# Turns of the identity in TensorE's pauses, and another order in the first expert tile

## The reference, cut to what matters

```python
def gat_layer(x, W, a_src, a_dst, bias, src, dst, heads, out_c, concat):
    h = (x @ W).reshape(n, heads, out_c)
    al_s, al_d = einsum(h, a_src), einsum(h, a_dst)
    e = leaky_relu(al_s[src] + al_d[dst], 0.2)
    ex = exp(e - segment_max(e, dst)[dst])
    alpha = ex / (segment_sum(ex, dst)[dst] + 1e-16)
    return segment_sum(h[src] * alpha, dst) + bias
...
x = x + gat_layer(elu(gat_layer(layernorm(x), heads=8, out_c=96)), heads=1, out_c=768)
# experts: 4 groups of 8, of which each token takes 2 groups and 4 experts in each
combine = softmax(top2(xf @ Wg + bg)) * softmax(top4(xf @ We + be))     # xf = layernorm(x)
y += (gelu(xf @ W1[g, e] + b1) @ W2[g, e] + b2) * combine[:, g, e]      # 768 -> 384 -> 768
```

## Time and profile before

| what | value |
|---|---|
| median of 3 runs | 1533.72 us (1532.51 to 1535.9) |
| profiled execution, its own time | 1535.3 us |
| its span, first to last instruction | 1533.3 us |
| mean granted clock of TensorE | 0.954 |
| busy: TensorE, DVE, ScalarE, POOL | 1362.5, 1160.9, 738.2, 503.2 us |

### The profile page before, as it was taken

The page is one execution under the profiler, slowest core; times in us unless marked ns, Lnnn a source line. Parts: engine busy times, 40 slices in busy tenths (PEclk is TensorE's granted clock), DMA queues, the critical chain, the costliest instruction groups (busy, mean ns, idle before and its releaser), DMA issues. The chain is left out here.

```text
span 1533.3 us, 31074 instructions
## 1 busy us (share of the span) xinstructions
PE 1362.5 (89%) x7643; PEld 1135.7 (74%) x7654; DVE 1160.9 (76%) x1823; ACT 738.2 (48%) x1171; POOL 503.2 (33%) x557
## 2 busy tenths in 40 slices
PE   6798888888778779889966999999999999999995
PEld 3555656633323339889966899999999999999995
DVE  6489999899999977858877576555566655888882
ACT  2565565255555552422224355444454544666662
POOL 1000000003333410032324454555555544655563
PEclk9999999799999989999976999999999999999998
DMA  6300001041222223233566887767778876889953
GB/s 231 137 18 9 18 21 68 18 177 61 72 94 72 68 54 130 62 104 105 125 183 219 238 215 197 192 163 162 169 197 211 200 193 154 214 268 271 257 126 49
DMA packets 102255, 211.68 MB, mean 138 GB/s; under 512 B 19318, under 2 KB 58486, under 8 KB 102082
## 3 DMA queue, kind: packets, MB, share of 16 engines
q1 hardware_dynamic: 79186, 142.06, 28.1%
q0 software_dynamic: 22240, 66.69, 21.7%
q10 hardware_dynamic: 784, 2.36, 0.4%
HBM read 164.14 MB, written 54.93 MB: 143 GB/s over the span
## 5 line engine op out<-in xcount | busy, mean ns | idle before, releaser
L976 PE MATMUL ps_o<-prob,h_head 128*97 128x512 f32 (+1 forms) x480 | 188.0, 529 | 51.5 <-DVE prob L918 51.5
L2050 POOL DMA_INDIRECT out_nodes<-y,to_index x92 | 159.7, 1736 | 148.3 <-issue 94.0
L2351 PE MATMUL ps_h<-e_hi,e_xt_hi 128*128 (+1 forms) x546 | 193.5, 354 | 7.1 <-ACT e_xt_hi L2169 3.7
L2336 PE MATMUL ps_y<-e_hi,e_ht_hi 128*128 (+1 forms) x546 | 193.1, 354 | 3.9 <-DVE e_ht_lo L2268 2.2
L976 PEld LDWEIGHTS ps_o<-prob,h_head 128*97 128x97 f32 x480 | 73.3, 165 | 165.6 <-issue 89.9
L2351 PE MATMUL ps_h<-e_lo,e_xt_hi 128*128 (+1 forms) x546 | 185.8, 340 | 0.0
L2336 PE MATMUL ps_y<-e_hi,e_ht_lo 128*128 (+1 forms) x546 | 184.8, 338 | 0.0
L2336 PE MATMUL ps_y<-e_lo,e_ht_hi 128*128 (+1 forms) x546 | 184.7, 338 | 0.0
L2234 DVE TENSOR_TENSOR e_lo<-raw,e_hi (+1 forms) x189 | 176.1, 952 | 7.6 <-ACT e_hi L2177 6.7
L2187 ACT ACTIVATE y<-ps_y,gate 128x768 f32 (+1 forms) x91 | 82.2, 903 | 196.7 <-DMA out_nodes<-y,to_index 100.4
L810 ACT ACTIVATE score<-score,al_col 128x1250 f32<-128x1250 f32 x80 | 106.0, 1335 | 98.7 <-DVE score L861 98.7
(11 more groups left out here) (346 smaller groups left out, 3037.7 us busy)
## 6 DMA issues: line engine op xcount, KB each, us to landing
raw<-in_ew SPq DMA_DIRECT2D x192, 384.0 KB, 5.8
w_room<-rel_dram SPq DMA_DIRECT2D x14, 640.0 KB, 4.5
b_all<-in_eb SPq DMA_DIRECT2D x32, 192.0 KB
al_src<-al_dram SPq DMA_DIRECT2D x1, 5000.0 KB, 14.8
xs<-in_x SPq DMA_DIRECT2D x5, 768.0 KB, 12.5
x_in_t<-in_x SPq DMA_DIRECT2D x10, 384.0 KB, 3.5
out_nodes<-x SPq DMA_DIRECT2D x10, 384.0 KB, 4.1
table<-xf SPq DMA_DIRECT2D x10, 384.0 KB, 2.6
```

The costliest lines, as they stand in the source:

```text
L976: turn = nc.tensor.matmul(ps_o[u][0:C1 + 1, c, 0:WID[c]], h_head[:, u, t, :], prob[:, t % 2, 512 * c:512 * c + WID[c]], start=(t == 0), st ...
L2050: nc.gpsimd.indirect_dma_start(out, bass.IndirectOffsetOnAxis(to_index[:, w:w + 1], 0), y[:, w, :], None, bounds_check=NP - 1, oob_is_err= ...
L2336: last = nc.tensor.matmul(ps_y[:, half, 0:HALF], a, b[:, bass.ds(u, 1), at:at + HALF].rearrange("p o d -> p (o d)"), start=(m == 0), stop= ...
L2351: nc.tensor.matmul(ps_h[:, 0:HID], xt_hi[:, c, :], b[:, bass.ds(e % 2, 1), c * HID:(c + 1) * HID] .rearrange("p o m -> p (o m)"), start=(c ...
```

## The change

A helper turns the identity into a PSUM bank that nothing reads. It is called at five places: 16 times in stage 1 after the first tile's products, 24 times before and 16 times behind the last `add_terms`, 8 times and 18 times in stage 5 around the last bias and the last list, and 3 times at the start of stage 6. In stage 6 the third list moves: on TensorE from behind the products of tile 0 to ahead of them, on DVE ahead of the low parts of expert 0's W2. DVE's first tile is written out in a function of its own: third list, match of the fourth, copy of tile 1, two low parts of W2, bias, `keep`, last low part of W2, split of tile 1, copy of tile 2, low part of the GELU, three low parts of expert 1's W1, match of the fifth.

```diff
+def turn_nothing(nc, s, to, times):
+    for n in range(times):
+        nc.tensor.transpose(to, s.ident[:, :], s.ident[:, :])
...
                 for t in range(NT):
+                    if t == 1:
+                        turn_nothing(nc, s, ps_al[:, 2, HALF:512], 16)
                     if t + 2 < NT:
                         turn_x(t + 2)
...
+                turn_nothing(nc, s, first_steep[:, 0:P], 24)
                 add_terms(H1 - 1, 1, last=True).then_inc(al_summed, 1)
+                turn_nothing(nc, s, first_steep[:, 0:P], 16)
...
                 turn_gates(NT - 1)
+                turn_nothing(nc, s, ps_l[:, 0:P], 8)
                 weigh_bias(NT - 1)
                 list_now(2)
+                turn_nothing(nc, s, ps_l[:, 0:P], 18)
...
+                def first_tile():
+                    keep_third()
+                    match(AHEAD - 1, 2, rows_made)
+                    keep_rows(1)
+                    weights(0, 1, (0, 1))
+                    dve.wait_ge(h_summed, 1)
+                    dve.wait_ge(b1_in, 16)
+                    nc.vector.tensor_tensor(h_in[:, :], ps_h[:, 0:HID], b1_all[:, 0, :], ALU.add).then_inc(biased, 1)
+                    keep(0)
+                    weights(0, 1, (2,))
+                    split_x(1)
+                    keep_rows(2)
+                    dve.wait_ge(h_hi_made, 1)
+                    nc.vector.tensor_tensor(ht_lo[:, :, :]..., ALU.subtract).then_inc(h_lo_made, 1)
+                    weights(1, 0, range(3))
+                    match(AHEAD, 3, rows_made)
+
                 def tile(k, e, which, start, last):
+                    if start:
+                        first_tile()
+                        return
...
                 split_x(0)
-                weights(0, 1, range(3))
                 over_tiles(dve, "dve_tiles", tile, alone)
...
                     if start:
-                        pe.wait_ge(third_made, 1)
-                        list_tokens(nc, s, ps_l).then_inc(third_listed, 1)
+                        pe.wait_ge(rows_made, 1)
+                        pe.wait_ge(third_kept, 2)
+                        list_tokens(nc, s, ps_l).then_inc(listed, 1)
                     turn_x(k + 1)
-                    if head and not last:
+                    if head and not last and not start:
                         pe.wait_ge(rows_made, e + 1)
-                        if start:
-                            pe.wait_ge(third_kept, 2)
                         list_tokens(nc, s, ps_l).then_inc(listed, 1)
...
                 turn_x(0)
+                pe.wait_ge(third_made, 1)
+                list_tokens(nc, s, ps_l).then_inc(third_listed, 1)
+                turn_nothing(nc, s, ps_y[:, 0, 0:P], 3)
                 n = over_tiles(pe, "pe_tiles", tile)
```

More of the change, by code:

```diff
@@ L2237, in weights @@
                                                 ALU.subtract).then_inc(made, 1)
+                def first_tile():
[11 more added lines that the diff above has]
+                    dve.wait_ge(h_hi_made, 1)
+                    nc.vector.tensor_tensor(ht_lo[:, :, :].rearrange("p k n -> p (k n)"), ps_t[:, 0:HID],
+                                            ht_hi[:, :, :].bitcast(F32).rearrange("p k n -> p (k n)"),
+                                            ALU.subtract).then_inc(h_lo_made, 1)
+                    weights(1, 0, range(3))
+                    match(AHEAD, 3, rows_made)
                 def tile(k, e, which, start, last):
+                    if start:
+                        first_tile()
+                        return
                     head = which == 0
@@ L2242, in tile @@
                         weights(e + 1, 0, (0, 1))
-                    if start:
-                        keep_rows(k + 1)
                     dve.wait_ge(h_summed, k + 1)
@@ L2247, in tile @@
                         dve.wait_ge(b1_in, 16 * e + 16)
-                    if not start:
-                        dve.wait_ge(gelued, k)
+                    dve.wait_ge(gelued, k)
                     nc.vector.tensor_tensor(h_in[:, :], ps_h[:, 0:HID],
@@ L2252, in tile @@
                                             ALU.add).then_inc(biased, 1)
-                    if start:
-                        keep_third()
-                        match(AHEAD - 1, 2, rows_made)
                     if which == 1:
```

## The result

| | before | after |
|---|---|---|
| median beside each other | 1533.25 us (8 executions) | 1524.78 us (8 executions, 1522.69 to 1530.57) |
| ratio, 95% interval | | 0.9948 [0.9935, 0.9961]: 6 to 10 us faster |
| profiled execution | 1535.3 us | 1525.1 us, span 1523.0 |
| mean granted clock | 0.954 | 0.966 |

The two profiled executions are 10.2 us apart, the medians 8.5. The execution on which the sum was made is 2.9 above that median. The changed kernel had 1524.7 in 14 executions.

The account below looks back on a forecast made before the run. TensorE bounds the kernel, losing time at half clock or where all engines wait in turn. Terms -1.6 - 4.1 + 0.1 - 0.85 = -6.5 us gave 1528.8 from the profile, 1528.0 by the median; forecast 1528.6, range 1526.0 to 1532.6.

Parts of the forecast that it names:

- second edit: End of the heads: 24 and 16 turns around the last terms save 4.1 us; bounds -6.3 and +1.6.
- Fourth edit: First expert tile: third list kept earlier and three turns save 0.85 us; bounds 0 and -2.7.
- POOL gets to that wait only after its second bias store: Expert start: POOL reaches its wait for the third list only at 826.29, limiting the gain to 0.85 us.
- should all come: Expert loop: the row of gathers up to TensorE's turn at 860.93 all come 0.85 us earlier.
- The barrier's -1.3: End of the heads: the next stage starts at about 570.8 instead of 572.05, 1.3 us earlier.
- The -2.5 and -0.3 behind it: Second layer's start: small turns and spread products at full clock save 2.5 us, big products behind them 0.3.
- rival 1: Second layer: its big products start at full clock too, a further 2 us off, 1526.6; chance 0.12.
- first edit: Node stage: 16 turns fill TensorE's 2.50 us wait and keep the clock, saving 1.6 us; bounds 0 and -1.7.
- third edit: Routing: 8 turns cost nothing, 18 make TensorE perhaps 0.3 late; +0.1 us, bounds 0 and +0.4.
- TensorE's drain last at a barrier: Sign of being wrong: TensorE's drain ends last at either barrier, the heads' end or the routing's end.
- rival 3: Heads' end: turns do not hold the clock, pauses cost as before, 1536.5 or 1534.9 us, slower; chance 0.08.
- rival 2: Heads' end: the cover fails, clock falls by 567, +1.6 in place of -4.1, 1534.5 or 1532.9; chance 0.14.

Follow-up runs that it names:

- POOL's zeros: Runs where POOL still writes the first zeros of y; the changed kernel with ScalarE writing them measured 1522.87 and 1523.97 us.
- the order alone: Kernel before with only the new order of the first expert tile, all five calls of turns left out: 1529.14 us, ratio 0.9981.
- the first edit alone: Kernel before plus only the 16 turns in the node stage (stage 1): 1529.54 us, ratio 0.9981.

## Why the prediction was wrong

| edit | forecast | alone, by the ratios |
|---|---|---|
| first | -1.6 | -2.9 (-0.8 to -5.1) |
| second | -4.1 | -2.0 (+0.2 to -4.1) |
| third | +0.1 | about 0 |
| fourth | -0.85 | -2.9 (-1.1 to -4.9) |
| sum | -6.5 | -7.8; the whole change -8.0 (-6.0 to -10.0) |

**The level.** The step "-6.5 us on the profiled execution, 1535.3: 1528.8" made most of the miss. The same -6.5 from 1532.4 gives 1525.9; of the 3.9 us between the forecast 1528.6 and 1524.7, 2.7 are this, or 1.9 if the eight executions beside the changed kernel (1533.25) are taken for the level. I had three times and a profile above two of them, and took the sum from the profile. The times of one kernel spread over 9 us.

**The sum.** That the forecast's -6.5 lies inside the measured -6.0 to -10.0 is luck: the second edit was priced some 2 us too high and the fourth some 2 us too low.

**Fourth edit.** The step that failed as a mechanism: "POOL gets to that wait only after its second bias store", at 826.29. Its engine ended there, its queue had passed the stores at 821.8, so with an early list most of the 4.3 us of queue steps go beside the stores. From the stage's start to the loop's first gate copy the four profiles with the late list ahead of POOL's steps have 13.9 to 15.0 us, nine with the new order (POOL's zeros) 9.6 to 10.6: 4.4 less on the mean. My other assumption, that the gathers behind it "should all come" as much earlier, failed the other way. From that copy to the one six gathers on it was 48.1 to 48.3 us with the late list and 48.8 to 51.7, mean 50.5, with the early one: 2.4 lost, 2.0 kept, which the measured 2.9 fits.

Part of that loss the traces show. In the first turn of the loop POOL waits for its own two bias stores to land before it goes on to the first addition to the output: 2.7 to 5.4 us in the nine profiles, none in three of those with the late list and 1.2 in the fourth. The turn takes 10.0 us on the mean in place of 9.2, and in six of the nine (the order alone, shown here, is one) POOL comes back to the gate copy without a wait for the gather.

```profile
828.55 1.27 POOL L2082 COPY to_index<-list_i 128x1 int32 x1 [2.63 <-DMA out_nodes<-bias_rows,node_i]
832.08 1.59 POOL L2056 DMA_INDIRECT out_nodes<-y,to_index  x1 [2.26 <-DMA out_nodes<-bias_rows,node_i]
833.89 0.21 POOL L2052 COPY gate<-landing 128x32 f32 x1 [0.22 <-issue]
```

In those six the landing of the bias stores is what comes late next. The other 1.6 us are lost in the turns behind it; why those gathers take longer is argued only: the load of the DMA engines (below).

**Second edit.** The barrier's -1.3 was right: 11.7 us from the turns of the sums to the next stage in all profiles with the 24 turns, 13.0 without, whether the 16 are there or not. The -2.5 and -0.3 behind it were too much. In the profile after, the small products and the big ones ran at full clock (rival 1 in its clock), but not in its time: TensorE then waits 2.25 us for `rel`, which waits for DVE's maxima, and those for the first mask. The first maximum before and after:

```profile
577.80 1.49 DVE L1157 CUSTOM_DVE_ANT_0 work<-work,ps_all 128x1280 bf16<-128x1280 bf16 x1 [2.56 <-PE ps_all L1251]
...
574.35 1.49 DVE L1167 CUSTOM_DVE_ANT_0 work<-work,ps_all 128x1280 bf16<-128x1280 bf16 x1 [2.16 <-DMA work<-mask_dram]
```

I had let DVE's maxima follow the spread rows alone, which held before. The big products, behind those rows, begin 2.94 us after the stage's first turn in place of 5.60; the first maximum begins 4.93 us after it in place of 5.71, so that 0.8 of the 2.7 come through. And in other executions the clock falls later. From the stage's first turn to DVE's second relation nine profiles with all 40 turns have 24.8 to 28.1 us, mean 26.0; five without have 25.5 to 27.2, mean 26.8. So 0.8 stays of my 2.8, with the barrier 2.1, as measured. The forecast expected the clock to fall once more around the two-row spread products, and it does in four of those nine, later in four, nowhere in one; what it missed is that the full price is not always paid without the turns either (25.5 in one of those five, the first edit alone, where the clock was back at 1.00 by 569.5 and fell again at 572.5). Its bound of -6.3 counts the -0.3 twice; the terms give -6.0.

**First and third.** The first is right in mechanism: the turns fit the wait, and the fall does not come. The 16 took 1.97 us, less than the 2.1 to 2.4 I had bounded. The measured 2.9 is more than the 1.6 of the rows, which lies inside its interval. The third edit showed no cost in time, and POOL still ends the block in the profile after, if by 0.4 us. But one sign of being wrong, TensorE's drain last at a barrier, came in five of the nine profiles with all 18 turns, in two of them by 0.8 and 0.95 us, above the bound of 0.4. In the changed kernel without the turns at the heads' end TensorE ends at 813.2, POOL at 812.25:

```profile
L1421 POOLq DRAIN  x1: 4850/4850/4850, 807.4 to 807.4; - x1
...
L1421 PEldq DRAIN  x1: 3400/3400/3400, 809.8 to 809.8; - x1
```

**Rivals.** That turns don't hold the clock (rival 3) is refuted here: granted 1.00 from 565 to 570 with 16 turns in it, and no fall in 13 profiles with the first edit. At the heads' end the last six terms took 4.46 to 4.50 us in all five profiles without the 24 turns, and about 1.05 + 1.5 us in all twelve with them. The Trainium skill's rule behind that rival (page "TensorE: Matmul & The Clock Gate", section "Part 4: PE-mode transpose": the full clock does not come on for transposes) disagrees with these numbers; the profile lists the turns as plain MATMUL. The cover at the heads' end did not fail in any of those twelve (rival 2).

One reading ahead of the sum was wrong: not each piece at half clock comes after a pause. In the kernel before TensorE was busy without a break from 275 on, from 281.16 with the products of two moving columns, and the clock fell at 285.5 all the same.

## What to carry to other kernels

An engine's row in the timeline is not its queue's: before a wait is said to stand behind an instruction, read when the queue itself passed it, above all on POOL, whose stores last microseconds. Take a sum from the median of many executions and not from the profiled one, and price a clock term over several profiles, since each shows one place of the fall among several. When a stage gets faster, ask what its consumer waits for besides it: here a mask load took some 2 us of the gain.

## What the runs showed of the hardware

Where the clock falls differs between executions of one kernel: of the changed kernel's two profiles one is at 1.00 from 565 to 586, the other at 0.50 from 579.2 to 582.5.

POOL's queue ran 4.5 us ahead of its engine through two indirect stores (821.8 against 826.29), and most of its 4.3 us of register steps went beside them: in the profile after, the gate copy behind those steps follows the second store by 1.2 us.

A gather's time went with what else the DMA engines moved; no run varied that load alone. In the profile after, the one issued at 841.70 is followed by its gate copy at 849.02, 7.3 us later; the one at 859.78 by its copy at 864.08, 4.3 us later. By stretches of that kernel, the DMA share is above 1 from 841 to 861, while the weights of the first experts load, and 0.54 behind:

```profile
841.00:851.00 10.00, 8.55 (x53) 7.71 (x51) 5.78 (x9) 2.64 (x5) 4.99 (x6) 1.00 1.06 351
851.00:861.00 10.00, 8.98 (x54) 8.65 (x55) 4.12 (x7) 3.73 (x6) 4.80 (x7) 1.00 1.03 330
861.00:871.00 10.00, 10.00 (x64) 9.89 (x63) 3.50 (x5) 2.80 (x5) 5.50 (x8) 1.00 0.54 102
```
